# First query tiles moved into the prologue of a latent-attention and feed-forward layer

## The reference

```
xn   = layernorm(x)
q    = rms_norm(xn @ wq_a.T, q_norm_w) @ wq_b.T        # 32 heads of 128 + 64 (rotary)
kv   = xn @ wkv_a.T                                    # 64 latents + 64 rotary keys
kv_up = rms_norm(kv[:, :64], kv_norm_w) @ wkv_b.T      # keys 128, values 128 of each head
scores = (q_nope . k_nope + rope(q_pe) . rope(k_pe)) / sqrt(192), causal
out  = softmax(scores) @ v @ wo.T
x    = x + layernorm(out)
x    = x + layernorm(swiglu_ffn(layernorm(x)))         # hidden 1376, integer weights
```

## Time and profile before

| | us |
|---|---|
| median of 3 runs (lowest, highest) | 1637.36 (1634.02, 1640.92) |
| the profiled execution | 1637.05 |
| its span | 1635.2 |
| PE busy in the span | 1534.8 (94%) |
| DVE busy | 1113.3 (68%) |
| ACT busy | 1107.0 (68%) |
| POOL busy | 953.3 (58%) |

### The profile page before, as it was taken

The page is one execution under the profiler, slowest core; times in us unless marked ns, Lnnn a source line. Parts: engine busy times, 40 slices in busy tenths (PEclk is TensorE's granted clock), DMA queues, the critical chain, the costliest instruction groups (busy, mean ns, idle before and its releaser), DMA issues.

```text
span 1635.2 us, 30457 instructions
## 1 busy us (share of the span) xinstructions
PE 1534.8 (94%) x10720; PEld 1282.8 (78%) x10720; DVE 1113.3 (68%) x2509; ACT 1107.0 (68%) x2203; POOL 953.3 (58%) x913
## 2 busy tenths in 40 slices
PE   6878899999999999998999999999986999999997
PEld 5756788778788787887888888888865778888775
DVE  6867778778787787886788788888864432323344
ACT  5677788788787787887888888878856543212134
POOL 2557777677676777777777777877722221111124
PEclk9899999999999999999999999999998999999999
DMA  8659999999999999999999999999987101101022
GB/s 281 233 149 210 185 211 187 205 182 203 211 185 207 179 206 199 193 198 202 182 192 192 181 199 179 197 195 173 199 214 259 59 27 38 40 1 41 1 78 103
DMA packets 661096, 268.85 MB, mean 164 GB/s; under 512 B 608432, under 2 KB 619184, under 8 KB 658768
## 3 DMA queue, kind: packets, MB, share of 16 engines
q1 hardware_dynamic: 660944, 266.90, 76.0%
HBM read 69.70 MB, written 29.36 MB: 61 GB/s over the span
## 4 chain that ended last, share of the span: by engine, by line
PE 73%; ACT 6%; DVE 6%; POOL 5%; DMA 5%; issue 3%; SPq 2%; POOLq 0%; ACTq 0%; DVEq 0%
PE s_ps L1052 20%; PE x_ps L163 16%; PE f_ps L163 13%; PE o_ps L1066 12%; PE fd_ps L163 6%; DMA weff_in<-weff 2%; PE x_ps L1075 2%; DMA qs<-q_raw 1%; POOL qf L1656 1%; POOL q_low L1663 1%; SPq L853 1%; POOL qs L1653 1%; ACT pk L1269 1%; PE x_ps L1083 1%; ACT s_ps L1261 1%
## 5 line engine op out<-in xcount | busy, mean ns | idle before, releaser
L1484 DVE CUSTOM_DVE_ANT_0 s_ps<-s_ps,far_sb 128x512 f32<-128x512 f32 (+7 forms) x512 | 390.8, 764 | 150.3 <-PE s_ps L1052 141.1
L1261 ACT ACTIVATE s_ps<-s_ps,nbias 128x512 f32<-128x512 f32 (+7 forms) x512 | 361.9, 715 | 86.5 <-DVE nbias L1484 86.3
L1497 DVE SCALAR_TENSOR_TENSOR pk<-s_ps,pk 128x512 f16<-128x512 f32 (+7 forms) x512 | 377.1, 753 | 31.7 <-ACT pk L1269 26.3
L1269 ACT ACTIVATE pk<-s_ps 128x512 f16<-128x512 f32 (+7 forms) x512 | 334.6, 654 | 15.1 <-DMA pt<-pk 8.9
L1066 PE MATMUL o_ps<-lat,pt 128*128 128x130 f16 x4608 | 307.4, 220 | 9.0 <-ACT o_norm L1278 8.9
L1066 PEld LDWEIGHTS o_ps<-lat,pt 128*128 128x128 f16 x4608 | 269.5, 97 | 54.2 <-issue 51.1
L1052 PE MATMUL s_ps<-k_high,q_high 128*128 128x512 f32 (+3 forms) x768 | 283.3, 369 | 11.6 <-POOL q_low L1663 7.2
L1653 POOL TENSOR_TENSOR qs<-qs,sin_q 64x512 f32<-64x512 f32 x128 | 164.4, 1284 | 189.8 <-DMA qs<-q_raw 183.5
L1052 PE MATMUL s_ps<-k_low,q_high 128*128 128x512 f32 (+3 forms) x768 | 257.6, 343 | 0.0
L1694 POOL TENSOR_TENSOR mid_low<-mid,mid_high 128x512 fp32r<-128x512 f32 (+1 forms) x44 | 56.8, 1290 | 302.1 <-ACT mid_high L1358 302.1
L1052 PE MATMUL s_ps<-k_high,q_low 128*128 128x512 f32 (+3 forms) x768 | 221.1, 342 | 0.0
(11 more groups left out here) (142 smaller groups left out, 2609.4 us busy)
## 6 DMA issues: line engine op xcount, KB each, us to landing
weff_in<-weff SPq DMA_DIRECT2D x64, 256.0 KB, 3.3
qs<-q_raw SPq DMA_DIRECT2D x256, 64.0 KB, 2.2
weff<-weff_sb SPq DMA_DIRECT2D x8, 1024.0 KB, 5.3
...
```

Source lines behind the costliest of these rows:

```text
L1261: e.activation(M.scores_of(i), M.scores_of(i), ACT.Exp, bias=M.nbias[:, i % 4:i % 4 + 1], scale=-1.0).then_inc(S.exp)
L1269: e.activation(M.halves_of(i)[:, :, 0, :], M.tiles_of(i), ACT.Copy, scale=P_SCALE).then_inc(S.p_high)
L1484: e.tensor_tensor_reduce(out=s, in0=s, in1=M.far_sb[:, SEQ - width:SEQ], scale=1.0, scalar=3e38, op0=ALU.add, op1=ALU.min, accum_out=M.nbi ...
L1497: e.scalar_tensor_tensor(out=M.halves_of(i)[:, :, 1, :], in0=M.tiles_of(i), scalar=P_SCALE, in1=M.halves_of(i)[:, :, 0, :], op0=ALU.mult, ...
```

## The change

Five things change.

1. `scores`, `minimum` and `exponential` of the tiles 0, 1 and 2 are given places in the prologue (`FIRST_TILES`); PE and DVE no longer wait for everything at `latents_over`. The wait moves to what needs it: `split_high(0)` on ACT, `split_low(0)` on DVE, `values(0)` and the first taker of `x_ps` on PE.
2. The second head's queries are made in the prologue as well, in the bank `f_ps` (`FIRST_QUERIES`), and their weights are loaded early (`SECOND_LOAD`).
3. The PSUM banks of the prologue are allocated in another order (`t_ps`, then `f_ps`, `a_ps`, `u_ps`), so that the slots of tiles 0, 1 and 2 lie over banks that come free early: slot 0 over `t_ps0`, slot 1 over `t_ps1` and `f_ps`, slot 2 over `a_ps0` and `a_ps1`.
4. `nbias` moves in SBUF to where the prologue has nothing.
5. A table `SHIFTS` moves 24 single steps by some places in the order (negative is earlier).

```diff
+FIRST_TILES = dict(scores=(18.1, 20.2, 20.4), minimum=(18.78, 21.0, 21.7), exponential=(18.8, 21.2, 21.8))
+N_FIRST = len(FIRST_TILES["scores"])
-FIRST_QUERIES = 0.12
-AFTER_FIRST = dict(queries_raw=0.33, queries_swap=-0.67, queries_turn=1.22)
+SECOND_LOAD = 8.9
+FIRST_QUERIES = dict(queries=(9.74, 13.74, 14.6, 16.9), queries_raw=(10.07, 14.07, 14.93, 17.23),
+                     queries_swap=(9.07, 13.07, 14.97, 17.3), queries_turn=(10.96, 14.96, 15.9, 20.0))
...
+    at(SECOND_LOAD, "queries_load", 1)
+    for what, places in FIRST_QUERIES.items():
+        for k, step in enumerate(places):
+            at(step, what, k // 2, k % 2)
+    for i in range(N_FIRST):
+        for what, places in FIRST_TILES.items():
+            at(places[i], what, i)
...
+SHIFTS = {
+    ('statistics', 1): -2, ('normalise', 3): -2, ('norm_keys', 0): 5, ('x_load', 7): -9,
+    ('latents_high', 0): -13, ('transpose_x', 6): -17, ('latents_low', 3): -2, ('rotary', 4): 2,
...
+    ('queries_load', 2): -5, ('split_high', 6): -4, ('minimum', 11): -6, ('scores', 17): 7,
...
+def shifted(turns):
+    return [turns[k] for k in sorted(range(len(turns)), key=lambda k: k + SHIFTS.get(turns[k], 0))]
...
 def queries(n, c):
...
-        if n == 0:
+        if n < 2:
             bank = M.f_ps[:, :]
             w.wait_ge(*free["f"])
             free["f"] = done
...
 def scores(i):
...
         if i >= NS:
             w.wait_ge(S.p_low, i - NS + 1)
+        elif i == 0:
+            w.wait_ge(S.xt_low, NT - 1)
+        elif i == 1:
+            w.wait_ge(S.xt_low, NT)
+            w.wait_ge(S.fold_low, STEPS)
+            w.wait_ge(S.q_raw, 4)
+        else:
+            w.wait_ge(S.qn, NT)
+            w.wait_ge(S.lat, NT)
```

More of the change, by code:

```diff
@@ L323, in __init__ @@
             self.lat2 = sb(attn, "lat2", [P, NT, LATW], F16)
-            sb(attn, "spare", [P, 2048 - NT * LATW // 2])
+            self.nbias = sb(attn, "nbias", [P, 4])
+            sb(attn, "spare", [P, 2044 - NT * LATW // 2])
             self.cos_q = sb(attn, "cos_q", [P, SEQ])
@@ L337, in __init__ @@
             with ExitStack() as ctx:
-                self.f_ps = pb(ctx, "f_ps")
                 self.latents(ctx, sb, pb)
@@ L368, in latents @@
         self.t_ps = [pb(ctx, f"t_ps{i}") for i in range(2)]
+        self.f_ps = pb(ctx, "f_ps")
         self.a_ps = [pb(ctx, f"a_ps{i}") for i in range(NA)]
@@ L487, in prologue_order @@
     at(max(TABLES_STEP, FOLD_FROM + AFTER_WEIGHTS["fold_out"]) + 0.1, "queries_load", 0)
-    for c in range(2):
-        step = (c + 1) * SEQ // 2 // P - 1 + AFTER_TILE["latents_low"] + FIRST_QUERIES
-        at(step, "queries", 0, c)
-        then(step, AFTER_FIRST, 0, c)
+    at(SECOND_LOAD, "queries_load", 1)
[5 more added lines that the diff above has]
+            at(places[i], what, i)
     for _, _, turn in sorted(turns):
@@ L496, in attention_order @@
 def attention_order(end):
-    yield "queries_load", 1
     yield ("latents_over",)
@@ L509, in attention_order @@
     for i in range(NJ):
-        at(i, "scores", i)
-        then(i, TILE_STEPS, i % JT, i)
+        if i >= N_FIRST:
+            at(i, "scores", i)
+        for what, places in TILE_STEPS.items():
+            if i >= N_FIRST or what not in FIRST_TILES:
+                at(i + places[i % JT], what, i)
     for u in range(NJ // 2):
@@ L518, in attention_order @@
     for n in range(1, NHEADS):
-        for c in range(2):
-            then(JT * (n - 1), QUERY_STEPS, c, n, c)
+        if n >= 2:
+            for c in range(2):
+                then(JT * (n - 1), QUERY_STEPS, c, n, c)
         if n + 1 < NHEADS:
@@ L723, in whole_order @@
     yield from end
-ORDER = [turn for turn in whole_order() if turn != PAUSE]
+SHIFTS = {
+    ('statistics', 1): -2, ('normalise', 3): -2, ('norm_keys', 0): 5, ('x_load', 7): -9,
+    ('latents_high', 0): -13, ('transpose_x', 6): -17, ('latents_low', 3): -2, ('rotary', 4): 2,
+    ('project', 11): 3, ('x_high', 14): -8, ('fold', 6): -3, ('halves', 12): -12,
+    ('squares', 15): -2, ('transpose_latents', 13): 5, ('exponential', 0): 4,
+    ('norm_queries', 14): -2, ('exponential', 2): 6, ('minimum', 4): 2, ('minimum', 5): 4,
+    ('queries_load', 2): -5, ('split_high', 6): -4, ('minimum', 11): -6, ('scores', 17): 7,
+    ('scores', 22): -3,
+}
+def shifted(turns):
+    return [turns[k] for k in sorted(range(len(turns)), key=lambda k: k + SHIFTS.get(turns[k], 0))]
+ORDER = shifted([turn for turn in whole_order() if turn != PAUSE])
 UNIT = {turn[1:]: n for n, turn in enumerate(t for t in ORDER if t[0] == "gate_up")}
@@ L954, in tensor_program @@
     w = Waits(e)
-    free = {"x": None, "f": None, "d": [None, None]}
+    free = {"x": (S.k_low, NT), "f": None, "d": [None, None]}
     turns = {"d": 0}
@@ L1030, in queries @@
         chain(e, bank, pairs).then_inc(S.q_mm)
-    def latents_over():
-        w.wait_ge(S.u_high, NT)
-        w.wait_ge(S.k_low, NT)
-        w.wait_ge(S.lat, NT)
-        for r in range(2):
-            w.wait_ge(S.weff_out[r], DMA * STEPS // 2)
     def scores(i):
@@ L1061, in values @@
             w.wait_ge(S.o_norm, u)
+        else:
+            w.wait_ge(S.k_low, NT)
         for i in (2 * u, 2 * u + 1):
@@ L1180, in tensor_program @@
     run(dict(transpose_x=transpose_x, project=project, transpose_latents=transpose_latents,
-             fold=fold, queries=queries, latents_over=latents_over, scores=scores, values=values,
+             fold=fold, queries=queries, scores=scores, values=values,
              outputs_turn=outputs_turn, fold_values=fold_values, output=output,
@@ L1245, in queries_raw @@
     def queries_raw(n, c):
-        bank = M.x_ps[:, :] if n else M.f_ps[:, :]
+        bank = M.x_ps[:, :] if n >= 2 else M.f_ps[:, :]
         w.wait_ge(S.q_mm, 2 * n + c + 1)
```

1 line of the change is left out of this document (removed).

## The result

| | median, us | runs |
|---|---|---|
| before | 1637.36 | 1631.95 to 1643.96, 19 |
| after | 1643.97 | 1636.10 to 1649.41, 19 |

The ratio is 1.0037 (95% interval 1.0025 to 1.0050): 0.4% slower, some 6 us. The forecast was 1637 and no change; the median is at the upper edge of the range of 1629 to 1644. The forecast took 0.5% as what can be told from no change; the interval is finer than that, and leaves out no change. The profiled execution after has a span of 1642.2 us against 1635.2.

What follows compares the result with a forecast made beforehand. PE and DMA fill the steady state, so the stretch before about 130 us decides. Parts 1 to 3 give 0, Part 4 -1.3, Part 5 +1.35: +0.05 on 1637.05, forecast 1637 us, range 1629 to 1644.

Steps and rivals of the forecast that it cites:

- Part 5: Early shifts in the prologue: statistics(1) -0.65 us, transpose_x(6) ahead of project(4) +2.0, the others 0; together +1.35.
- Rival C: At 45 to 54 us: PE's short gaps around 40 us close, the clock's fall disappears; 1634 us, chance 0.18.
- Part 1: PE before its last fold: head 1's queries, waits for weights, scores(0) and q_raw add 6.0 us, none hidden.
- Part 2: Last weights_high to last latents: 7.3 us instead of 6.6, with table load and exponential(0) 1.95, no drain.
- Part 3: Behind the latents: split_high(2) starts at 104.8 us against 105.14, 0.3 earlier, so the early tiles gain nothing.
- Part 4: Behind the latents: head 1's early queries give back 1.8 us, minimum(11) waiting for scores(11) costs 0.5; together -1.3.
- Rival A: Up to the latents' end: PE's waits absorb the added steps, last k_low near 96 to 97; about 1629 us, chance 0.22.
- Rival B: POOL holds the prologue: halves(12) after 90 us, PE stalls with its clock down; about 1645 us, chance 0.10.

Runs made afterwards that it cites:

- e1: Changed kernel with transpose_x(6) back where it stood before, all else as changed: 1635.47 us, ratio 0.9990 to the kernel before.
- e2: Kernel before with transpose_x(6) alone moved 17 turns earlier: 1640.13 us, ratio 1.0027 to the kernel before.
- e4: Changed kernel with head 1's two query groups back behind the latents: 1641.04 us, ratio 1.0026 to the kernel before.
- e5: Changed kernel with the three first tiles back behind the latents: 1639.22 us, ratio 1.0013 to the kernel before.
- e6: Changed kernel with nine dummy matmuls behind scores(1): 1641.24 us, ratio 1.0032 to the kernel before.
- e9: Changed kernel with transpose_x(6) back and exponential(0), with its table load, behind latents_high(15): 1632.58 us, ratio 0.9977 to the kernel before.
- e13: Changed kernel with transpose_x(6) back, 4 dummy matmuls ahead of tile 8's transposes and 9 behind scores(1): 1633.69 us, ratio 0.9986 to the kernel before.
- e17: Changed kernel with transpose_x(6) and the three first tiles back, 4 dummy matmuls ahead of tile 8's transposes: 1634.82 us, ratio 0.9990 to the kernel before.
- e18: e9 with dummy matmuls, 5 ahead of tile 6's transposes, 4 ahead of tile 8's, 3 behind scores(1): 1631.80 us, ratio 0.9970 to the kernel before.
- e19: Kernel before with the early shifts of the change except transpose_x(6): 1634.07 us, ratio 0.9976 to the kernel before.
- e3: Changed kernel without the whole table of shifts; first tiles, head 1's queries and banks as changed: 1635.02 us, ratio 0.9996 to the kernel before.
- e12: Kernel before with dummy matmuls, 6 ahead of tile 6's transposes and 4 ahead of tile 8's: 1637.90 us, ratio 1.0007 to the kernel before.
- e10: Changed kernel with dummy matmuls, 8 ahead of tile 6's transposes and 6 ahead of tile 8's: 1636.82 us, ratio 1.0010 to the kernel before.
- e14: Changed kernel with 8 dummy matmuls ahead of tile 6's transposes alone: 1637.82 us, ratio 1.0010 to the kernel before.
- e21: Kernel before with the early shifts of the change, transpose_x(6) included: 1638.41 us, ratio 1.0007 to the kernel before.
- e20: Kernel before with transpose_x(6) 17 turns earlier and 8 dummy matmuls ahead of its transposes: 1639.66 us, ratio 1.0012 to the kernel before.

## Why the prediction was wrong

**The step that failed is Part 5, the term of transpose_x(6).** It had +2.0 us, with 4.2 as its bound; the shift costs 7.7 us in the changed kernel (e1) and 4.4 in the kernel before (e2). The place was right (PE waits for xn of tile 6, clock down behind it), and so was the wait: 3.5 us were reckoned, and e2, e4, e5 and e6 show 3.80 to 3.82; it is 2.27 in the profile of the changed kernel, where 20 to 30 us ran at 0.87 of the clock. What stands behind the wait was priced wrong. Sorting the profiles of the table by this shift and by the clock of 50 to 60 us gives A as:

| | clock 0.83 or more | clock 0.77 or less |
|---|---|---|
| transpose_x(6) late | 53.2 (e1, e9, e13, e17, e18, e19; 51.0 to 55.2) | 55.5 (before, e3, e12; 55.1 to 55.7) |
| transpose_x(6) early | 56.2 (e10, e14, e21; 55.3 to 57.4) | 60.0 (after, e2, e4, e5, e6, e20; 58.6 to 61.2) |

So the moved order costs 3.0 us where the clock of 50 to 60 us stays up, and 3.8 more where it is down. The 3.8 are not the clock alone: all profiles of the last cell also have a slow normalise(8) (0.66 to 1.61 us), those of the others 0.55 to 0.57.

Three profiles show it stepwise. From the first transposes to fold 2 it takes 23.0 us in e1, 25.2 in e14 and 26.6 in the changed kernel: 2.2 us of queue, where the prediction had 1.6 (34.80 to 36.4), and 1.5 of project(4) at half clock, for which it had nothing in the fold's time. From fold 2 to queries(0,1) it takes 29.9, 30.1 and 33.7 us. Of these 3.6, 1.1 are normalise(8) beside POOL (1.61 for 0.55 us); 2.5 lie behind queries(0,0), most of them in fold 3 and the matmuls ahead of it at half clock (fold 3 takes 3.65 us for 1.97). Sum 7.4 us of A, against 7.7 by the ratios.

The prediction said that PE recovers over project(4). It did not; project(4) was what had filled the wait, and it came back behind the wait at half speed. And it priced one fall of the clock and neither the next, in the stretch that is weak anyway (45 to 54 us), nor the meeting of DVE and POOL that the delay brings about. That meeting was partly chance: with the same delay it did not happen in e21, where rotary(3) came later. Why POOL's data came later there is open.

**The other terms of Part 5** were too small the other way. The early shifts without transpose_x(6), of which statistics(1) was priced at -0.65 and the rest at 0 within 1, gave 2.2 us of A and 3 to 4 in the time (e19; from 1 to 7). What statistics(1) gave by itself isn't shown: the first transposes start at 12.62 before and at 11.44 after, but at 11.74 in e2, which lacks this shift, and at 12.45 in e6, which has it. Where the shifts gain is seen at the first half of head 0's queries, queries(0,0): PE waits 1.09 us for k_low there before and in e3, 0.18 in e1 and e19, and fold 3 behind it takes 3.65 us in the former and 2.09 and 1.98 in the latter. These two errors have opposite signs and cancel in part. That the median came out inside the range at all is luck, of these two signs.

**Rival C** was half true: with these shifts and transpose_x(6) late the clock of 45 to 54 us is 0.81 (e1) in place of 0.50, and the kernel before with them is where C put it (1634; e19 has 1634.07). The wait that closed is the one for k_low, and it is the shifts and not PE's being late that closed it. transpose_x(6) took that away: 0.66 after.

**Part 1 was right** in its own stretch. Its mark (94 to 96 us, with 1.35 on top) was missed at 98.58 by what Part 5 missed. From queries(0,1) to the last weights_high: 21.0 us before, 26.9 after, +5.9 for the 6.0 of the sum; PE's two waits for weff_sb are 1.17 and 1.08 us for the 1.0 taken. **Part 2** was near, with the last k_low at 106.13 in place of 102 plus 1.35 for the same reason: weights_high to k_low went from 6.3 to 7.55 us, +1.3 for +0.7, and e9 shows the load and exponential as 2.06 us. The table load is followed by the exponential 0.02 us after its end here too (100.39 + 1.28, 101.69), no drain of 1.38 us in either kernel. **Part 3** held in relation, not by its mark of 105 to 106: split_high of tiles 1 and 2 is one stretch from 108.90 us, so that of tile 2 starts near 109.5, 4.4 later than 105.14 with 4.0 us brought from ahead of it (71.72 against 67.73); the half clock behind the latents, bounded by 0.8, costs about 1.2 (e6, e13). **Part 4**: PE's wait for q_low of head 1 is gone. scores(17) was to come 1 us earlier against split_high(2) and came 2.5 later (136.29 less 109.5, against 129.44 less 105.14): its own wait of 0.78 us is gone, but the first fold_values, now ahead of it, waits 1.38 us for ACT's q_raw, which the prediction had at nothing. The -1.3 can't be told from nothing in the medians. Parts 1 to 4 together: -1.3 in the sum, and 1635.02 against 1636.03, ratio 0.9996, without any shift (e3, which lacks the shifts of minimum(11) and scores(17)).

**Rival A** is refuted: the last k_low came at 106.13, not before 99. **Rival B** did not happen, though its mark came up: halves(12) was at 90.15, after 90, but less the 4.0 us brought from ahead that is 86.2, as early as the 86.7 reckoned, and between 86 and 124 us PE has no wait for POOL.

What stays open: what the early tiles and the place of head 1's queries are worth at the end (e4, e5 and e17 don't settle it), how much of the 2.1 us between e1 and e9 is real, and how much of the 3.6 us behind fold 2 would stay if normalise(8) alone, or the clock alone, were mended. No run parts the two.
